# Mixture of experts: the second down weights split earlier, and two weight loads issued ahead of the row loads

## What is computed

```python
rn = (xf - mu) * jax.lax.rsqrt(var + EPS) * ln_gamma + ln_beta
probs = jax.nn.softmax(rn @ gate_w.T, axis=-1)
rw, sel = jax.lax.top_k(probs, K)                                  # K = 2
comb = jnp.sum(jax.nn.one_hot(sel, E, dtype=xf.dtype) * rw[..., None], axis=1)
h = jax.nn.gelu(jnp.einsum('nc,efc->enf', xf, w1), approximate=False)
y = jnp.einsum('enf,ecf->enc', h, w2)
out = jnp.einsum('enc,ne->nc', y, comb)
```

## Time and profile before

| | |
|---|---|
| median of three runs | 954.24 us (953.05 to 955.04) |
| the profiled execution | 951.88 us, span 950.0 us |
| busy share: PE, DVE, ACT, POOL | 91%, 71%, 56%, 41% |
| the mixture's block | from 747 us to the end |
| w_raw<-in_w, loads of expert weights | 30 of 2048 KB, median 16.1 us to landing |
| share of the chain that ended last, loads of weights | 7% |

### The profile page before, as it was taken

How to read it: one execution, slowest core, us unless ns; L and a number is a source line. 1 busy time by engine, 2 the same in 40 slices (tenths; PEclk the granted TensorE clock), 3 DMA queues, 4 the chain that set the end, 5 groups by cost and what they waited for, 6 DMA issues and landing times. The chain is left out here.

```text
span 950.0 us, 24410 instructions
## 1 busy us (share of the span) xinstructions
PE 866.1 (91%) x10317; PEld 607.8 (64%) x10317; DVE 679.1 (71%) x1022; ACT 528.2 (56%) x811; POOL 385.0 (41%) x294
## 2 busy tenths in 40 slices
PE   5998999999999999999999999987786499999995
PEld 2464776776766867757767757763444387776663
DVE  7765788656688555679666556676778759999893
ACT  3643454565354564454555545551567359988883
POOL 1130765345566345656444545555230032111112
PEclk9999999999999999999999999999987789999999
DMA  9354121352221232212333202206502839999993
GB/s 336 110 160 118 36 68 40 118 145 70 58 57 47 80 123 79 69 38 50 93 108 98 66 21 52 72 22 264 204 1 99 307 106 341 400 403 399 403 371 41
DMA packets 48453, 134.66 MB, mean 142 GB/s; under 512 B 9893, under 2 KB 11813, under 8 KB 44493
## 3 DMA queue, kind: packets, MB, share of 16 engines
q1 hardware_dynamic: 45354, 126.81, 39.6%
q0 software_dynamic: 2800, 6.04, 3.1%
q10 hardware_dynamic: 192, 0.26, 0.1%
HBM read 95.03 MB, written 11.31 MB: 112 GB/s over the span
## 5 line engine op out<-in xcount | busy, mean ns | idle before, releaser
L469 POOL TENSOR_TENSOR acc_pool<-acc_pool,pT 128x1024 f32<-128x1024 f32 x90 | 212.0, 2356 | 144.8 <-ACT pT L741 143.2
L741 ACT ACTIVATE pT<-ps_s 128x1024 f32<-128x1024 f32 x124 | 126.6, 1021 | 192.8 <-PE ps_s L925 192.7
L575 DVE TENSOR_REDUCE mpart<-ps_b 128x1 f32<-128x512 f32 x256 | 173.7, 685 | 74.2 <-PE ps_b L905 73.4
L889 PE MATMUL ps_a<-wv_hi,cT_hi 128*128 128x128 f16 x1024 | 183.5, 219 | 0.4 <-ACT kbias L658 0.4
L891 PE MATMUL ps_a<-wv_hi,cT_lo 128*128 128x128 f16 x1024 | 182.7, 219 | 0.0
L890 PE MATMUL ps_a<-wv_lo,cT_hi 128*128 128x128 f16 x1024 | 182.5, 219 | 0.0
L570 DVE TENSOR_TENSOR k_lo<-k_f,k_hi 128x512 f16<-128x512 f32 x64 | 77.1, 1204 | 65.9 <-ACT k_hi L714 65.9
L889 PEld LDWEIGHTS ps_a<-wv_hi,cT_hi 128*128 128x128 f16 x1024 | 99.8, 97 | 8.3 <-issue 5.9
L890 PEld LDWEIGHTS ps_a<-wv_lo,cT_hi 128*128 128x128 f16 x1024 | 100.2, 98 | 7.2
L925 PEld LDWEIGHTS ps_s<-q_stack,k_stack 101*128 101x128 f16 x992 | 72.0, 97 | 47.8 <-ACT pT L741 16.0
L925 PE MATMUL ps_s<-q_stack,k_stack 101*128 101x128 f16 x992 | 93.0, 219 | 9.8 <-ACT pT L741 8.9
(11 more groups left out here) (277 smaller groups left out, 1843.1 us busy)
## 6 DMA issues: line engine op xcount, KB each, us to landing
w_raw<-in_w SPq DMA_DIRECT2D x30, 2048.0 KB, 16.1
raw<-in_context SPq DMA_DIRECT2D x16, 1024.0 KB, 5.6
k_stack<-k_hi SPq DMA_DIRECT2D x252, 64.0 KB, 2.0
k_stack<-k_lo SPq DMA_DIRECT2D x128, 64.0 KB, 2.0
slots_in<-a_zeros SPq DMA_DIRECT2D x1, 3855.0 KB, 13.1
rows_in<-slots_in SPq DMA_DIRECT2D x15, 257.0 KB, 15.9
q_stack<-k_stack SPq DMA_DIRECT2D x12, 128.0 KB, 2.4
x_sb<-in_x SPq DMA_DIRECT2D x2, 512.0 KB, 4.3
```

What stands on the lines that cost most here:

```text
L469: nc.gpsimd.tensor_tensor(acc_pool[:, :], pT[:, 0, :] if p == 1 else acc_pool[:, :], pT[:, p % PT, :], ALU.add).then_inc(pool_add, 1)
L575: nc.vector.tensor_reduce(mpart[:, j, kb:kb + 1], bank_at(step)[:, :], AX.X, ALU.max).then_inc(p1_max, 1)
L741: nc.scalar.activation(pT[:, p % PT, :], scores(w, p)[:, :], ACT.Exp, scale=SM_SCALE).then_inc(exp_done, 1)
L889: nc.tensor.matmul(to, cT_hi[:, c, keys], t.wv_hi[:, c, col], start=(c == 0), stop=False)
```

## The change

SP issues w2 of tile 3 and w1 of tile 4 before it waits for the scatters of rows, not in its pass through the tiles. Both loads wait for the low part of the weights that their buffer holds. w2 of tile 1 is therefore split earlier: ScalarE's two halves stand behind its last copy of the router, and VectorE's halves stand behind the router's last operation and behind the first tile's first `h_lo` and `x_low`. No operation is added or dropped.

```diff
+            w2_load(3)
+            w1_load(4)
             sp.wait_ge(sent, 16 * 2 * NB)
             for k in (*range(EARLY, ROWS_AHEAD), *range(EARLY)):
                 rows_load(k)
@@
-                if 4 <= k + 3 < TILES:
+                if 5 <= k + 3 < TILES:
                     w1_load(k + 3)
-                if 3 <= k + 2 < TILES:
+                if 4 <= k + 2 < TILES:
                     w2_load(k + 2)
@@ VectorE
-            def w2_low(k):
-                for i in range(PARTS):
+            def w2_low(k, parts=range(PARTS)):
+                for i in parts:
...
+            w2_low(1, (0,))
             for k in range(TILES):
                 if 2 <= k + 1 < TILES:
                     w1_low(k + 1)
...
                     if i == (0 if k + 1 < EARLY else 1) and k + 1 < TILES:
                         x_low(k + 1)
+                    if (k, i) == (0, 0):
+                        w2_low(1, (1,))
                 if k + 2 < EARLY:
                     pick_rows(k + 2)
-                if k:
+                if k >= 2:
                     w2_low(k)
@@ ScalarE
             for b in range(1, NB):
                 second_copy(b)
+            w2_high(1)
             x_high(0)
...
-                if k:
+                if k >= 2:
                     w2_high(k)
```

## The result

The changed kernel takes 962.99 us (median of 6 executions, 960.29 to 966.15) where the kernel before takes 954.64 beside it (953.05 to 958.03): a ratio of 1.0086, 95% interval 1.0062 to 1.0110. It is slower by 8.4 us. 956.9 was forecast, with 961.0 as the upper end: the sign is right, the size is not. The profiled execution took 960.29, its span is 958.5; before it was 950.0, so the two traces differ by 8.5 us. Each lies some 2.7 us under the median of its kernel, so they can be compared line by line.

What follows compares the result with a forecast made beforehand. The mixture was taken as bound by TensorE, and from tile 9 by loads. Terms -5.7 (loads), +5.3 (stand), +2.6 (clock) and +0.5 (result scatters) sum to +2.7 on 954.24: 956.9 us, range 949.6 to 961.0.

Steps and rivals of the forecast that it cites:

- (a): Two ScalarE splits move into its 7.05 us pause ahead of 763.58: cost nothing, or 3.7 without the pause.
- (c): Two loads issued early give TensorE a lead beyond the eleven tiles left: gain 5.7 us, bounds 4.2 and 5.7.
- (b): Two VectorE splits move forward between router and h_lo work: cost nothing, or 4.5 us without that cover.
- (d): SP's list: waiting for w1_low(2) costs at most 0.4 us; later row loads priced at nothing, upper bound 1.
- (e): Moved VectorE splits hold POOL's row scatters; the eighth lands 7.5 us later, TensorE stands 5.3 (bounds 0.9 and 8.5).
- (f): TensorE's clock after the stand: 5.3 us of work at half speed loses 2.6 us, bounds 0 and 4.
- (g): Result scatters on POOL, one behind another, lag at the end: 0.5 us, bounds 0 and 5.3.
- R4: Rival: TensorE's stand comes and the lead in loads is lost too: +8.4 us, 962.6; chance 0.08.
- R1: Rival: the sixth row scatter slips in ahead of w1_low(2), TensorE stands 1.5 us: -3.7, 950.5; chance 0.22.
- R2: Rival: held POOL scatters end with the VectorE operation, not 0.85 behind; stand 0.8 us: -4.4, 949.8; chance 0.05.
- R3: Rival: VectorE splits do not delay POOL's scatters at all: -5.2 us, 949.0; chance 0.08.

Runs made afterwards that it cites:

- the loads alone: Changed kernel with VectorE's two moved splits cut to 8 columns of one row block, loads still early: 953.83 us, -1.14 against the kernel before.
- the change with the reads first: Changed kernel with SP's reading of the later tiles' experts moved ahead of the two early loads: 959.55 us, +4.58 against the kernel before.
- splits alone: Kernel before with the splits of w2 of tile 1 moved as in the change, loads left in place: 954.92 us, -0.05 (ratio 1.0003).
- one load early, reads first: Changed kernel with tile 4's w1 load at its old place and SP's expert reads ahead of the row loads: 951.80 us, -1.59 against the kernel before.

## Why the prediction was wrong in size

(a) and (c) stood: ScalarE's two splits fit into its pause, and the late waits of 5.7 went in full (eleven tiles of 10.98), at the upper bound that was taken. TensorE's lateness was not needed for that: the loads alone, with a stand of 2.3, have late waits of 0.2. The working of (c) says that the lead lasts for more than the eleven tiles left, but its numbers leave no margin (10.4 against 10.4).

(b) "moving them gains nothing there but lets the next loads go" was wrong in one thing: the place they left let w1_low(3) come forward from 789.1 to 782.03, in this trace into the eighth scatter. The experiment that put it back gained nothing, and the change with the reads first shows the loss without that hold.

(d) SP's wait for VectorE cost nothing by itself, as priced. What the prediction took as given, the 5.5 us between the first row load and tile 3's, turned out to be the cheap part to remove: 3.8 us of the change's loss by the medians, 2.0 to 3.9 of gain without the change.

(e) The mechanism was right (scatters held, rows late, a stand at tile 3's transposes, then no gap) and the landing too small. From the first scatter's start to the eighth's end 17.0 was forecast, 18.5 measured in the changed kernel's trace: the working held four scatters by splits and three for a little by h_lo; in the trace splits hold five, the eighth among them. But the other traces with both splits moved have 15.2 to 17.4, so the hold was sized about right, and the 1.5 is this execution's. The landing is the miss: "I take half of the 5.7 between: 2.9" on top of 1.8; 6.4 behind the end in place of 4.7 in this trace, and up to 11.3 in the experiments, where the outer bound was 7.5. The price came from half-way between two rows of result scatters, with and without loads beside them; the runs with both loads early show that a held scatter can wait until the load that it meets has nearly drained. The working looked at the eighth scatter beside w1_load(4) alone and put at nothing what w2_load(3) does to the scatters ahead of it; they land 10.7 us behind issue. The two errors in this trace, 1.5 and 1.7, make up nearly all of the 3.3 us by which the transposes came later than the forecast 5.3 (the first scatter starts 0.5 earlier, and the way from the first row load to the transposes is 0.5 longer).

The Trainium skill (DMA: Bandwidth & Descriptors, section "Queues, rings and completion order") says that each engine takes turns between its queues by whole packets of several descriptors. The trace has 46 packets of the scatters beside 83 of a load in 4 us, so both queues were served; how many make a turn, and whether the size of a load's packets sets the landing, no run here shows, and it stays open.

(f) 2.6 was forecast, 1.5 measured (7.09 against 5.63 between the hole and tile 3): 2.9 us of work at half speed, where 5.3 was taken.

(g) is the step that failed outright: 0.5 forecast, 4.1 measured. It set a landing of 11.0 against tiles of 10.98, which leaves the ring no lag to speak of. But a link of the ring is the landing and 0.8 more, 11.75 in the kernel before, so by the same rows it loses some 0.8 us a tile once tiles come 10.98 apart; in the changed kernel links take 11.7 to 15.1. The page's group of these scatters, shown above, says otherwise for the kernel before already: of 139.1 us of POOL's idle time ahead of them, 114.4 are waits for its own previous scatter. Through the whole loaded stretch the ring was later than the evictions. Only the last two scatters wait for an eviction, idle 5.15 and 5.53, where one that waits for the ring alone idles 3.85 (the scatter of 952.45 above): 1.3 + 1.7 = 3.0 us to spare. A gain of 5.7 at TensorE could not have come through it whole. In the changed kernel the ring's scatters also take longer to land at first (13.2 against 11.0).

The measured time lies close to R4's 962.6, and R4 is wrong all the same: it kept the late waits, which went. R1 needed an eighth scatter that is done ahead of w1_load(4)'s packets; it ended 6.2 us behind that load's issue. R2 needed scatters that end with the split that held them; four ended 0.85 behind. R3 needed none held; five were. The misses of (e), (f) and (g), +3.3, -1.1 and +3.6, make up the difference between the forecast +2.7 and the 8.5 us of the traces.

## What to carry to other kernels

Before pricing a gain on the engine that bounds a kernel, look at every serial chain that runs beside it (here a ring of transfers, each waiting for the one before) and ask how much it could be early: what is beyond that is lost, whatever the engine gains. Two small delays on the way to one transfer are not priced one by one when the first pushes it into the traffic that the second brings. And before starting a large transfer early, look for what its own queue does in front of it: seven register reads of SP, moved out of the way, cut the late waits from 5.7 to 0.7 us, and the time by 2.0 to 3.9 in two runs.

## What the runs showed of the hardware

A scatter of rows that POOL starts inside one of VectorE's splits ends 0.85 us behind it: 772.70 against 771.85, 777.54 against 776.69, 779.75 against 778.90 and 785.17 against 784.32 in the changed kernel. The first, which takes 1.25 even beside no VectorE operation (767.11 before), ends 1.12 behind its split (769.57 against 768.45). The Trainium skill (SBUF — State Buffer, section "A bandwidth-pool intuition that's wrong") has the loser blocked until the operation's end plus about 115 ns, for a copy on VectorE; the runs agree on the block and show a longer tail, nearly the whole instruction (0.97 alone, as the seventh scatter of the changed kernel shows with 0.98).

Stands of TensorE and the clock behind them: with 1.0 us (splits alone) and 2.3 (loads alone) ahead of the transposes the granted clock stayed at 1.00; with 2.6 (one load early, reads first) it was at half over 794.9 to 798.3; in the changed kernel, with 11.1, over 793.3 to 803.5. A stand of 2.5 us ahead of the last down product, which all fourteen traces have, was followed by 3.4 us at half the clock in seven of them and by none in the other seven, the kernel before and the changed kernel among these; where it came, the last eviction ended 20.8 to 21.0 us behind tile 14's start, and 19.3 to 19.4 where it did not. What decides it there no run shows. The forecast had found no stand with a lower clock behind it in the trace of before, and priced the climb from a start at the lower level.
